# Sums of squares as two rounded products for six more units of batches 0 and 1, with two x buffers from batch 1 on

## The reference, cut to what matters

```
h = modulate(rmsnorm(x, g1, D), scale_msa, shift_msa)
q, k, v = split(h @ Wqkv.T + bqkv)
q = rmsnorm(q, gq, hd) * hd ** (-0.5)      # per head, over its 32 values
k = rmsnorm(k, gk, hd)
o = softmax(q @ k.T) @ v
x = x + gate_msa * (o @ Wproj.T + bproj)
h = gelu(modulate(rmsnorm(x, g2, D), scale_mlp, shift_mlp) @ Wfc1.T + bfc1)
x = x + gate_mlp * (h @ Wfc2.T + bfc2)
```

## Time and profile before

| what | value |
|---|---|
| median of 3 runs | 1768.58 us (1768.52 to 1770.08) |
| the profiled execution | 1769.43 us, span 1767.6 us |
| PE busy | 1720.9 us, 97% of the span |
| DVE busy | 1054.2 us, 60% |
| ACT busy | 976.1 us, 55% |
| POOL busy | 391.5 us, 22% |
| granted TensorE clock, mean | 0.996 |

### The profile page before, as it was taken

How to read it: one execution, slowest core, us unless ns; L and a number is a source line. 1 busy time by engine, 2 the same in 40 slices (tenths; PEclk the granted TensorE clock), 3 DMA queues, 4 the chain that set the end, 5 groups by cost and what they waited for, 6 DMA issues and landing times.

```text
span 1767.6 us, 23560 instructions
## 1 busy us (share of the span) xinstructions
PE 1720.9 (97%) x8476; PEld 1151.0 (65%) x8476; DVE 1054.2 (60%) x1269; ACT 976.1 (55%) x1272; POOL 391.5 (22%) x303
## 2 busy tenths in 40 slices
PE   8999999999999999999998999999999999999999
PEld 5655555555555555554334878888888888888887
DVE  6678887889998899888777454142322324142301
ACT  4577777798888889889886432222222212221221
POOL 3001110111111111000150233333333333333332
PEclk9999999999999999999999999999999999999999
DMA  8554554555565555556765202010020202010000
GB/s 289 130 156 127 144 145 114 136 150 143 143 160 127 152 143 132 150 138 158 179 144 209 60 18 66 19 54 24 18 65 6 65 18 65 18 53 24 18 18 24
DMA packets 122245, 176.96 MB, mean 100 GB/s; under 512 B 29568, under 2 KB 43904, under 8 KB 121136
## 3 DMA queue, kind: packets, MB, share of 16 engines
q1 hardware_dynamic: 119648, 163.75, 34.8%
q10 hardware_dynamic: 1712, 9.47, 1.4%
q0 software_dynamic: 800, 2.62, 0.5%
HBM read 124.87 MB, written 50.92 MB: 99 GB/s over the span
## 4 chain that ended last, share of the span: by engine, by line
PE 79%; DVE 11%; ACT 5%; issue 3%; DMA 1%; SPq 1%; ACTq 0%; POOL 0%; DVEq 0%
PE scores L1470 20%; PE scores L564 10%; PE pv L1487 10%; PE gemm L1487 10%; PE pv L581 9%; PE gemm L660 7%; DVE sums L895 7%; PE pv L1442 4%; PE gemm L673 4%; ACT probs L808 4%; PE aux L598 2%; DVE raw L920 1%; DMA wstage<-in_wqkvT 1%; PE aux L1457 1%; PE aux L612 1%
## 5 line engine op out<-in xcount | busy, mean ns | idle before, releaser
L808 ACT ACTIVATE probs<-scores,shift 128x1024 f32<-128x1024 f32 x512 | 550.5, 1114 | 125.7 <-PE scores L564 116.7
L895 DVE TENSOR_TENSOR sums<-sums,probs 128x2048 f32<-128x2048 f32 x186 | 439.1, 2361 | 26.9 <-ACT probs L808 24.0
L564 PE MATMUL scores<-q_stack,k_stack 128*128 128x512 f32 x1024 | 348.9, 425 | 9.5 <-ACT probs L808 7.9
L1470 PE MATMUL scores<-w_hi,act_parts 128*128 128x512 f32 x1016 | 316.3, 393 | 0.0
L564 PEld LDWEIGHTS scores<-q_stack,k_stack 128*128 128x128 f32 x1024 | 172.1, 188 | 196.1 <-ACT probs L808 90.8
L1402 POOL TENSOR_TENSOR act_parts<-act_full,act_parts 128x512 fp32r<-128x512 f32 x127 | 169.7, 1336 | 478.6 <-ACT act_parts L1333 478.6
L581 PE MATMUL pv<-probs,v 128*32 128x512 f32 x2048 | 257.8, 601 | 0.4 <-ACT probs L808 0.4
L1470 PEld LDWEIGHTS scores<-w_hi,act_parts 128*128 128x128 f32 x1016 | 189.9, 189 | 38.7
L1333 ACT ACTIVATE act_parts<-act_full 128x512 fp32r<-128x512 f32 x127 | 80.3, 632 | 221.3 <-PE scores L1470 220.4
L1470 PE MATMUL scores<-w_lo,act_parts 128*128 128x512 f32 x508 | 198.4, 391 | 0.0
L1546 DVE TENSOR_TENSOR y_next<-pv,p_bias 128x512 f32<-128x512 f32 x28 | 19.3, 691 | 299.7 <-PE pv L1442 299.7
(11 more groups left out here) (197 smaller groups left out, 2062.2 us busy)
## 6 DMA issues: line engine op xcount, KB each, us to landing
k_stack<-parts_scratch SPq DMA_DIRECT2D x128, 256.0 KB, 4.9
q_stack<-parts_scratch SPq DMA_DIRECT2D x128, 256.0 KB, 5.4
parts_scratch<-parts SPq DMA_DIRECT2D x62, 512.0 KB, 3.1
inverse<-inverse_scratch SPq DMA_DIRECT2D x128, 64.0 KB, 2.1
heads_out<-o_out SPq DMA_DIRECT2D x32, 256.0 KB, 4.5
out<-result SPq DMA_DIRECT2D x30, 256.0 KB, 2.0
heads<-heads_out SPq DMA_DIRECT2D x28, 256.0 KB, 4.0
x_tile<-in_x SPq DMA_DIRECT2D x28, 256.0 KB, 2.8
```

The lines of the kernel that those rows point to most:

```text
L564: mm = nc.tensor.matmul(scores[p][:, i, :], k_stack[s][:, h, j * P:(j + 1) * P], q_stack[half][:, h, :], start=True, stop=True)
L808: nc.scalar.activation(probs[L % RING][:, 2 * p:2 * p + 2, :], scores[p][:], ACT.Exp, bias=small["shift"][:]).then_inc(exp_done, 1)
L895: nc.vector.tensor_tensor(sums[:], a[:], probs[l % RING][:], ALU.add).then_inc(added, 1)
L1470: mm = nc.tensor.matmul(acc[t], parts_of(c, m)[:, b, t * P:(t + 1) * P], w2[a][:, m, :], start=(m == 0 and i == 0), stop=(m == NM - 1 and ...
```

## The change

It does three things.

1. HALVED becomes a list. Beside the units from 24 on it takes those of batches 0 and 1 from unit 4 on whose later sum still fits: units 14, 15, 17, 18, 20 and 21. Their sums have the second form (a rounded square on ACT, a subtraction on DVE, two fast matmuls on PE in place of one float32 matmul), and their steps move: unit 14 from 26 to 28, 15 from 28 to 29, 17 from 36 to 37, 18 from 38 to 40, 20 from 44 to 46, 21 from 46 to 47. Logarithm, inverse root, multiplication and parts move by the same number of steps. All other sums keep their steps.
2. The split into parts of these six units stays on DVE alone; the bound for ACT's share is now called HANDED (24).
3. Since `squares_hi` lies in the memory of the third x buffer and is now used from step 25 on, the x tiles use two buffers from batch 1 (tile 8) on. The loads of steps 20, 22, 24, 28, 32, 40 and 46 carry tiles 10, 11, 12, 13, 14, 16 and 17 (11, 12, 13, 14, 15, 17 and 16 before); tile 15 gets a slot at step 36, and the load of tile 10 at step 10 goes.

```diff
 def x_home(n):
-    return n % XS if n < 2 * NT else n % 2
-
-def x_owner(n):
-
-    if n < 2 * NT:
-        return n - XS
-    return 4 * NT - 1 - n if n < 2 * NT + 2 else n - 2
-
-XLOAD_AT = {TURN[x_owner(n)] + 1: n for n in range(NT + XS, B * NT)}
-XLOAD_AT.update({NT + n: NT + n for n in range(XS)})
+    return n % XS if n < NT else n % 2
+
+XLOAD_AT = {TURN[n - 2] + 1: n for n in range(NT + 2, B * NT)}
+XLOAD_AT.update({NT + n: NT + n for n in range(2)})
...
-HALVED = 6 * NU
-SUM_AT = {}
-for n, step in enumerate(UNIT_END):
-    step += 1 if step < 0 else 2 if n < HALVED else 3
+HANDED = 6 * NU
+HALVED, SUM_AT = [], {}
+
+def sum_step(step, wait):
+
+    step += wait
     while step in SUM_AT or step in ROWS_AT or step in TURN_AT and step >= 0:
         step += 1
-    SUM_AT[step] = n
-SQ_LOW_AT = {step + 2: n for n, step in enumerate(UNIT_END) if n >= HALVED}
+    return step
+
+for n, step in enumerate(UNIT_END):
+    at = sum_step(step, 3)
+    if n >= HANDED or n >= NU and at + 2 <= UNIT_END[n + 2] and at > max(SUM_AT):
+        HALVED.append(n)
+    else:
+        at = sum_step(step, 1 if step < 0 else 2)
+    SUM_AT[at] = n
+SQ_LOW_AT = {step + 2: n for n, step in enumerate(UNIT_END) if n in HALVED}
...
         def load_x(n):
             if n >= NT:
-                sp.wait_ge(turned, x_owner(n) + 1)
+                sp.wait_ge(turned, max(n - 1, XS))
...
         def sum_squares(n):
-            if n < HALVED:
+            if n not in HALVED:
...
             nc.scalar.activation(squares[:], raw[n % 2][:], ACT.Square).then_inc(sq_done, 1)
-            if n >= HALVED:
-                if n == HALVED:
-                    act.wait_ge(turned, 2 * NT - 1)
+            if n in HALVED:
+                if n == HALVED[0]:
+                    act.wait_ge(turned, XS)
                 nc.scalar.activation(squares_hi[:], raw[n % 2][:], ACT.Square).then_inc(sq_hi_done, 1)
```

More of the change, by code:

```diff
@@ L149 @@
 RAW_AT = {step + 1: n for n, step in enumerate(UNIT_END)}
-HALVED = 6 * NU
-SUM_AT = {}
-for n, step in enumerate(UNIT_END):
-    step += 1 if step < 0 else 2 if n < HALVED else 3
+HANDED = 6 * NU
+HALVED, SUM_AT = [], {}
+def sum_step(step, wait):
+    step += wait
     while step in SUM_AT or step in ROWS_AT or step in TURN_AT and step >= 0:
         step += 1
-    SUM_AT[step] = n
-SQ_LOW_AT = {step + 2: n for n, step in enumerate(UNIT_END) if n >= HALVED}
+    return step
[7 more added lines that the diff above has]
+SQ_LOW_AT = {step + 2: n for n, step in enumerate(UNIT_END) if n in HALVED}
 INV_AT, FIN_AT = ({step + after: n for step, n in SUM_AT.items()} for after in (1, 2))
-LOW_AT = {step + (n >= HALVED): n for step, n in FIN_AT.items()}
+LOW_AT = {step + (n >= HANDED): n for step, n in FIN_AT.items()}
 LEAN = -(-max(FILL) // NT)
@@ L613, in sum_squares @@
             else:
-                pe.wait_ge(sq_lo_done, n - HALVED + 1)
+                pe.wait_ge(sq_lo_done, HALVED.index(n) + 1)
                 aux_free()
@@ L850, in scalar @@
                 square(RAW_AT[L])
-            if L in FIN_AT and FIN_AT[L] >= HALVED:
+            if L in FIN_AT and FIN_AT[L] >= HANDED:
                 high_part(FIN_AT[L])
@@ L980, in make_parts @@
             unit_norm(n)
-            if n >= HALVED:
+            if n >= HANDED:
                 return
@@ L995, in square_low @@
             dve.wait_ge(sq_done, n + 1)
-            dve.wait_ge(sq_hi_done, n - HALVED + 1)
+            dve.wait_ge(sq_hi_done, HALVED.index(n) + 1)
             nc.vector.tensor_tensor(squares_lo[:], squares[:], full(squares_hi[:]), ALU.subtract).then_inc(sq_lo_done, 1)
@@ L1002, in vector @@
             parts_first = L in FIN_AT and (L < 0 or L in RAW_AT and RAW_AT[L] == FIN_AT[L] + 2)
-            low_first = L in LOW_AT and LOW_AT[L] >= HALVED and RAW_AT.get(L) == LOW_AT[L] + 2
+            low_first = L in LOW_AT and LOW_AT[L] >= HANDED and RAW_AT.get(L) == LOW_AT[L] + 2
             if low_first:
@@ L1023, in vector @@
                 square_low(SQ_LOW_AT[L])
-            if L in LOW_AT and LOW_AT[L] >= HALVED and not low_first:
+            if L in LOW_AT and LOW_AT[L] >= HANDED and not low_first:
                 low_part(LOW_AT[L])
```

## The result

The changed kernel takes 1779.41 us (median of 4 runs, 1778.23 to 1781.5) against 1769.12 us of the kernel before (4 runs): ratio 1.0058, 95% interval 1.0046 to 1.0071. It is slower by 10.3 us, or 8.1 to 12.6 by the interval. The profiled execution took 1778.23 us, its span is 1776.4 us, 8.8 more than the span before.

The account below looks back on a forecast made before the run. PE holds 79% of the path, but DVE ends PE's waits in the touched stage. Walks of +4.6, 0 and +4.4 sum to +9.0 on the 1768.58 us median, less 0.1: 1777.5 us, range 1772.5 to 1781.

Parts of the forecast that it names:

- Where the six old sums stand: End of steps 26 to 46, 172 to 259 us: none on the path by itself; cheaper sums save 1.7 to 2.4 us at most.
- First wait: Steps 28 and 46: squares 15 and 21 wait for PE's later sums, holding exponentials; next step's scores come 3.0 us later.
- Second wait: Logarithms 15 and 21 wait for DVE's multiplication, holding exponentials of steps 30 and 48; PE stands 1.7 us in the first pair.
- third wait: Unnamed in the prediction: DVE's late parts 15 ahead of other moves, within the walk's delay of row sums at step 33.
- The sign of being wrong: Prediction wrong if PE's gaps in steps 29, 31, 47 and 49 add up to less than 5 us; two other signs.
- the walk: Step-by-step timing of the moved sums from profile rows: +4.6 first pair, about 0 middle, +4.4 last pair, sum +9.0 us.
- Row sums of step 33: End of the first pair's walk: they start at 205.6 instead of 200.98 us, +4.6.
- The sums by place: Units 14 and 15 +4.6 us, middle units 17 and 18 about 0 (-0.5 to +1), units 20 and 21 +4.4.
- The added work: Per unit one ACT square (0.615 us), mostly hidden, and one DVE subtraction (0.686); ahead of raw 15, 18, 21 about +0.6 each.
- The x buffers: Two buffers cost 0: tightest is tile 10, with 8.5 us against a median of 3.8 from issue to landing.
- The clock: Four new PE gaps: the skill's rule gives 16 us total, the row with a 2.58 us wait leaves 9; row taken.
- half clock: Rival: half rate after one or two gaps, +1.7 or +3.4 us; after all four 1784.3 us; chance 0.14.

Follow-up runs that it names:

- buffers: Kernel before with two x buffers from batch 1 on and nothing else of the change: ratio 0.9999 (0.999 to 1.0008), median 1769.95 us.
- squares-later kernel: Changed kernel with squares 15 and 21 and their subtractions one step later, behind the exponentials of steps 28 and 46: ratio 1.0043, 7.6 us slower than before.
- first pair alone: Kernel before with two x buffers and only units 14 and 15 in the second form with later sums: ratio 1.0027, 4.8 us slower.
- late sums in the old form: Changed kernel with six sums in their later steps but still float32, without rounded square or subtraction: ratio 1.0043, 7.6 us slower than before.
- parts-behind kernel: Changed kernel with squares and sums 15 and 21 one step later, and DVE's unit 15 work behind raw 16 in step 33: 1.0015, 2.7 us slower than before.
- first ten units: Kernel before with two x buffers and only units 4 to 13 in the second form, sums in old steps: ratio 1.0013, 2.3 us slower.

## Why the prediction was right

It gave 1777.5 us within 1772.5 to 1781, slower with 0.87. Point by point:

- **Where the six old sums stand.** They were off the path, so their cheaper form saves nothing by itself. Shown by the kernel with the new form in the old steps: from step 25 to 50 its marks never gain more than 0.1 us on "buffers", and it ends 3.0 us slower.
- **First wait, square behind the sum of a later step.** Scores of step 29 forecast at 187.1, measured 187.03; PE's stand forecast 2.2, measured 2.30; exponentials forecast from 186.0, measured 185.89. The squares-later kernel shows the cause: without this wait the pairs cost 1.8 and 2.2 us less at the marks, net of the new waits for the subtraction.
- **Second wait, logarithm behind DVE's multiplication.** PE was to get the first exponential of step 30 at 196.1; its scores of step 31 start at 196.05. In the changed kernel PE does not stand for it: a half-clock stretch had slowed its work from 188 us on, so that step 30 began 4.2 us late, against 2.6 in the kernel with the first pair alone, while step 31 began 4.4 us late in both (counted from step 25). Where no such stretch came, the wait is as forecast: 1.66 us against 1.7 with the first pair alone, 1.24 twice with the late sums in the old form. Taking it away alone won nothing, because with the later sum the third wait was larger (2.15 us, about 1.0 of it beside GpSimd's subtraction).
- **The sign of being wrong.** PE's gaps in steps 29, 31, 47 and 49 were to be 5 us or more. The profiled execution has two of 2.30 us for exponentials, 4.6 in all, so by its own letter the sign was met. The gaps missing in steps 31 and 49 are those that slower matmuls filled: with the late sums in the old form they add up to 6.0. The sign should have named the marks, not the gaps.
- **The row behind the second wait.** I took the 2.58 us of the earlier trace rows for this mechanism. It is another: PE waits there for a move to raw, and DVE has parts 22 ahead of that move, which is the third wait's form. In the kernel before:

```profile
284.79 0.69 DVE L977 SCALAR_TENSOR_TENSOR parts<-raw,parts 128x512 fp32r<-128x512 f32 x1
285.59 0.75 DVE L920 TENSOR_SCALAR raw<-gemm,qk_bias 128x512 f32<-128x512 f32 x1
```

  The size of the second wait came from the walk, and that was sound; the row gave it no support.
- **Row sums of step 33.** Forecast at 205.6, measured 205.40. The walk had this third wait in its last line, as the step from +3.2 to +4.6, without naming it a mechanism or a rival; the parts-behind kernel shows that it is one.
- **The sums by place.** 4.6, 0, 4.4 forecast; 4.5, 0.5, 4.3 in the trace, and 4.8, 0.9, 4.6 by the ratios of the kernels with one group alone. The step that was off by a little is the middle. Step 38 begins 1.1 us late as forecast and step 40 only 0.2; the 0.4 that stays comes at step 41. The sum of unit 18 at the end of step 40 was to be covered by the wait for raw 19 (0.96 us in "buffers"); in the changed kernel PE waits 0.79 there for the additions behind the row sums instead.
- **The added work.** I counted three subtractions with 0.6 us each ahead of bank moves, 1.8 us, and three others with nothing. That PE waits for two of these three moves already was misread: in the kernel before it waits only for that of raw 18 (0.6 us, step 37; the other two waits for raw in the earlier trace rows stand in steps 41 and 49). In the old steps the work costs 3.0 us over all six, twice what I expected there. On top of the late sums it costs 1.7 us at the marks (9.4 against 7.7 for the late sums in the old form), near the 1.8 of the walk; by the ratios it is 2.7, with intervals that overlap. There the parts of units 14, 17 and 20 no longer stand ahead of V, which may be why the other three subtractions cost nothing; it was not tested. So the walk's 1.8 fits only in company with the late steps.
- **The x buffers.** 0, shown by the kernel with them alone (within 1.8 us either way).
- **The clock.** I took the row over the rule. For the clock itself that was the weaker choice, for the time the better one. Two half-clock stretches came, one in each pair:

```profile
186.00:192.00 6.00, 4.96 (x18) 3.21 (x22) 4.62 (x5) 6.00 (x8) 2.30 (x1) 0.72 0.17 45
...
266.00:271.00 5.00, 4.63 (x16) 3.44 (x20) 4.05 (x5) 5.00 (x7) 2.30 (x1) 0.66 0.67 136
```

The granted clock is the third number from the end, 0.72 and 0.66. Each came with a 2.30 us wait. That idle gaps bring back half rate is what the Trainium skill says (TensorE: Matmul & The Clock Gate, "HAM oscillation — how this bites in real kernels"), for a kernel with longer gaps than these. The two stretches here agree with it; the first pair alone, with the same 2.30 us wait and no such stretch before step 50, does not. The price of 1.7 us for each was wrong. The first pair costs the same 4.5 us with the stretch and without, since PE had to wait for the exponentials anyway. Where nothing waits behind, as in the middle of the kernel with that group alone, a stretch does cost 1.6 (2.2 against 0.5 us). So the rival "half clock" happened in the clock and hardly in the time: the 9.4 us of the marks come near the 9.0 of the walk, and not near the 16 of the rule.

What stays open: the 10.3 us of the medians against 8.8 between the two profiled spans; the forecast was 8.9 above the median it started from. The marks account for 9.4 in steps 25 to 50; half-clock stretches that differ from one execution to the next could make the rest, which was not separated.

## What to carry to other kernels

When an instruction is moved later, look at every in-order queue that waits for it, and ask what stands behind the waiter: here a one-tile buffer (`squares`) tied ACT's next square to a sum that had moved past it, and two exponentials stood behind the square. The sum is cheap, its lateness was not: 0.3 to 0.4 us saved, 4.5 us lost in each pair. Before trading work from one engine to two others, check which engine the path runs through at that place; here the trade went from PE to DVE just where DVE ended every wait of PE. And walk a moved step through to the point where the queues meet again; the third wait was five steps away from the first.

## What was not expected of the hardware

- The place of a half-clock stretch is not fixed by the kernel's waits alone. After the 2.58 us wait in step 53 the kernel before shows none, and neither does the changed kernel. The kernel with the x buffers alone has the same wait and runs the stretch behind it at a granted clock of 0.72:

```profile
286.00:292.00 6.00, 6.00 (x26) 2.60 (x27) 5.64 (x5) 2.76 (x4) 0.00 (x0) 0.72 0.45 133
```

  Eleven of the twelve experiments have such a stretch that begins between 287 and 300 us. One execution's trace without it proved little. The reverse case is step 23: PE waits 1.6 to 1.8 us there in all fourteen traces, and only those of the kernel before and of one experiment (the first ten units) have a stretch behind it.
- Such a stretch moved the marks by 1.6 us where PE was the path (between steps 53 and 54 in "buffers", of which 1.0 was made good by step 60, where PE waits 0.39 us for a move to raw and in the kernel before 1.39) and by nothing that the marks show where PE had to wait next.
